# Attention on one core: where the row products stand among the score products of a block

## The reference

```
x: (4, 1024, 1024), D = 1024, 32 heads of 32 columns
h      = layernorm(x) * (1 + ca) + sa
q,k,v  = h @ Wq.T + bq, h @ Wk.T + bk, h @ Wv.T + bv      # split in 32 heads
scores = einsum('bhqd,bhkd->bhqk', q, k) / sqrt(32)
scores = where(causal, scores, -inf)
att    = softmax(scores, axis=-1)
x      = x + ga * (einsum('bhqk,bhkd->bhqd', att, v) @ Wo.T + bo)
h      = layernorm(x) * (1 + cb) + sb
x      = x + gb * experts(h)                               # top 2 of 4, rank 16
```

## Time and profile before

| | |
|---|---|
| three executions | 3041.66, 3042.66, 3043.70 us |
| profiled execution, its own time | 3043.05 us |
| its span, first to last instruction | 3041.3 us |
| granted PE clock from 1302 to 2407 us (in `attend`) | 1.00 |
| in the same 1105 us: PE busy | 1066.65 us |
| DVE, ACT, POOL busy | 737.84, 622.82, 797.86 us |

### The profile page before, as it was taken

The page is one execution under the profiler, slowest core; times in us unless marked ns, Lnnn a source line. Parts: engine busy times, 40 slices in busy tenths (PEclk is TensorE's granted clock), DMA queues, the critical chain, the costliest instruction groups (busy, mean ns, idle before and its releaser), DMA issues. The chain is left out here.

```text
span 3041.3 us, 42552 instructions
## 1 busy us (share of the span) xinstructions
PE 2872.8 (94%) x16692; PEld 2026.8 (67%) x16692; DVE 1528.6 (50%) x3062; ACT 1047.4 (34%) x1443; POOL 1384.0 (46%) x702
## 2 busy tenths in 40 slices
PE   4999999999999999799999999999999959999997
PEld 2788888888888888555555555555555447777775
DVE  4232223222313122366666666666666447777875
ACT  1322321132213111255555555555555521211211
POOL 2322322242225111367776677776777722433342
PEclk8999999999999999899999999999999979999997
DMA  7444343343336444445544444444455163345341
GB/s 240 181 161 161 127 180 111 111 149 128 132 144 194 176 166 151 125 109 120 121 113 112 116 112 112 113 113 112 117 119 120 48 210 110 111 141 156 120 139 42
DMA packets 153935, 404.91 MB, mean 133 GB/s; under 512 B 21756, under 2 KB 57012, under 8 KB 152712
## 3 DMA queue, kind: packets, MB, share of 16 engines
q1 hardware_dynamic: 123416, 292.05, 28.0%
q10 hardware_dynamic: 30320, 110.15, 16.2%
HBM read 270.41 MB, written 131.20 MB: 132 GB/s over the span
## 5 line engine op out<-in xcount | busy, mean ns | idle before, releaser
L1082 ACT ACTIVATE prob<-ps_s 128x1024 f32<-128x1024 f32 (+3 forms) x768 | 598.6, 812 | 471.6 <-PE ps_s L1201 396.1
L782 PE MATMUL ps_u<-h_hi,w_hi 128*128 128x512 f32 x1536 | 620.6, 404 | 1.9 <-POOL h_lo L550 1.6
L782 PE MATMUL ps_u<-h_lo,w_hi 128*128 128x512 f32 x1536 | 608.8, 396 | 0.0
L782 PE MATMUL ps_u<-h_hi,w_lo 128*128 128x512 f32 x1536 | 608.8, 396 | 0.0
L1038 POOL TENSOR_TENSOR added<-added,prob 128x2048 f32<-128x2048 f32 (+1 forms) x128 | 550.0, 4297 | 10.8 <-ACT prob L1082 10.5
L544 POOL TENSOR_TENSOR w_lo<-w_raw,w_hi 128x1024 fp32r<-128x1024 f32 x93 | 222.8, 2396 | 490.2 <-ACT w_hi L612 490.2
L673 DVE SCALAR_TENSOR_TENSOR qk_lo<-ps_u,bias_col,qk_hi 128x512 fp32r<-128x512 f32 x128 | 96.0, 750 | 595.4 <-ACT qk_hi L588 595.4
L1125 DVE TENSOR_REDUCE part_high<-ps_r 128x1 f32<-128x512 f32 x496 | 329.8, 686 | 83.9 <-PE ps_r L1171 75.4
L1121 DVE CUSTOM_DVE_ANT_0 ps_r<-ps_r,row_mask 128x384 f32<-128x384 f32 (+1 forms) x500 | 309.1, 632 | 80.4 <-PE ps_r L1171 68.4
L1171 PE MATMUL ps_r<-k_st,q_st 96*128 96x512 f32 (+1 forms) x1008 | 322.7, 374 | 18.8 <-DMA v_sb<-v_tok 9.2
L782 PEld LDWEIGHTS ps_u<-h_lo,w_hi 128*128 128x128 f32 x1536 | 289.3, 188 | 70.2
(11 more groups left out here) (196 smaller groups left out, 3602.4 us busy)
## 6 DMA issues: line engine op xcount, KB each, us to landing
w_raw<-w_cols SPq DMA_DIRECT2D x72, 512.0 KB, 6.3
qk_split<-qk_hi SPq DMA_DIRECT2D x64, 512.0 KB, 2.6
qk_split<-qk_lo SPq DMA_DIRECT2D x64, 512.0 KB, 4.1
q_st<-qk_split ACTq DMA_DIRECT2D x60, 512.0 KB, 7.6
k_st<-qk_split ACTq DMA_DIRECT2D x60, 512.0 KB, 13.8
xn<-in_L_attn_x SPq DMA_DIRECT2D x8, 2048.0 KB, 13.0
v_tok<-v_out SPq DMA_DIRECT2D x32, 512.0 KB, 4.4
wm<-in_L_wmod SPq DMA_DIRECT2D x8, 2048.0 KB, 7.9
```

Source lines behind the costliest of these rows:

```text
L782: last = nc.tensor.matmul(ps_u[u % 2][:], w[:, m, k], h[:, k, tok], start=k == 0 and j == 0, stop=k == KT - 1 and j == 2)
L1082: nc.scalar.activation(prob[:, buffer_of(t, k), 2 * pair:2 * pair + 2, off:], ps_s[pair][:, :, off:], ACT.Exp, scale=SCALE).then_inc(exp_d ...
```

## The change

The table is another one. Nothing stands in front of the first score pair of a block now; two row products stand in front of the second, of the third and of the fourth; one stands behind the fourth, as before.

```
-    SHARE = (2, 2, 1, 1, 1)
+    SHARE = (0, 2, 2, 2, 1)
```

## The result

The changed kernel takes 3066.47 us (median of six, 3062.24 to 3069.15) against 3042.16 for the kernel before on the same chips (six, 3037.78 to 3044.19). The ratio is 1.0082, interval 1.0069 to 1.0095: slower by 24 us. The forecast was slower, 3061, and the range of 3044 to 3079 holds the result. The profiled execution took 3066.32 us by its own time, with a span of 3064.3.

The account below looks back on a forecast made before the run. Transfers bound block 5, an ACT chain block 2, PE's stream with stops the rest. Terms 0.68 - 0.21 - 0.10 - 0.45 + 0 + 0.70 = +0.62, taken as 0.6 over 30 groups: +18 us, 3061; range 3044 to 3079.

Parts of the forecast that it names:

- Block 3, +0.68: Block 3: waits for DVE's banks make the last row product 1.02 us later, less 0.34 of saved front: +0.68 a group.
- Block 5, +0.70: Block 5: the turn moves behind the first score pair, its 4.56 us transfer chain stays: 5.15 instead of 4.45, +0.70.
- Block 2, 0: Block 2: the ACT chain starts with the first score pair and keeps its length, so no change.
- Block 4, -0.21: Block 4: fourth score pair at 3.50 instead of 3.24, +0.26, less block 5's saved front of 0.47: -0.21 a group.
- block 0, -0.10: Block 0: fourth score pair at 3.09 instead of 2.83, +0.26, less a saved front of 0.36: -0.10 a group.
- Block 1, -0.45: Block 1: fourth score pair stays where ACT lets it go, some 0.02 later, less a saved front of 0.47: -0.45.
- A: Rival, chance 0.10: row products fill PE's holes and DVE keeps up; -0.94 us a group, -28 us, 3015.
- C: Rival, chance 0.13: DVE ends last everywhere, so blocks 0, 1 and 4 save nothing; 1.38 a group, +41 us, 3084.
- B: Rival, chance 0.13: blocks 0, 1 and 4 save their whole fronts, blocks 3 and 5 lose 0.68 and 0.70; +0.08, 3045.
- The transfers: Block 5: the later turn might meet less traffic and win back up to 0.22 a group, some 7 us; left out of sum.

Follow-up runs that it names:

- DVE relieved: Changed kernel with DVE taking single row products' maxima over half of their columns only: 3023.12 us, ratio to the kernel before 0.9936.
- block 3 alone new: Kernel before, with the new table (0, 2, 2, 2, 1) in block 3 only: 3073.54 us, ratio 1.0106.
- block 5 as it was: Changed kernel, with the old table (2, 2, 1, 1, 1) back in block 5: 3063.15 us, ratio to the kernel before 1.0068.
- half DVE work in the kernel before: Kernel before, with DVE taking single row products' maxima over half of their columns: 3030.90 us, ratio 0.9969.
- block 3 as it was: Changed kernel, with the old table (2, 2, 1, 1, 1) back in block 3: 3038.92 us, ratio to the kernel before 0.9986.
- block 5 alone new: Kernel before, with the new table (0, 2, 2, 2, 1) in block 5 only: 3047.09 us, ratio 1.0020.
- the fastest one: Changed kernel with table (1, 2, 2, 1, 1), the turn one place earlier, and own tables for blocks 1, 2 and 3: 2992.78 us, ratio to before 0.9846.
- two transfers: Changed kernel, sending the upper chunk's shift with two transfers instead of four from group 4 on: 3059.34 us, ratio to the kernel before 1.0055.

## Why the prediction was right, point by point

- **Block 3, +0.68: +0.71.** The timetable from DVE's 0.60 us a product gave r4 at 1.51, r6 at 2.60 and S3 at 2.71 after S0; measured 1.52, 2.60 and 2.71. Undone, done alone, and with DVE relieved, it moves as the three banks say. The +0.71 holds the 0.34 of block 4's front; block 3's table by itself costs 1.0 (block 3 alone new).
- **Block 5, +0.70: +0.62 in the mean**, 4.45 to 5.15 between the groups shown. The turn comes 0.60 behind S0 instead of 0.11 ahead, and 4.55 us of DVE, SP and transfer follow. What I didn't see is how near PE's own work was behind it (0.34 us).
- **Block 2, 0: -0.02.** Its chain over ACT starts at S0, but it doesn't quite keep its length: the first exponential starts 0.85 us after S0 instead of 0.98, S1 comes 0.93 behind S0 instead of 1.05, and the median group is 6.57 long instead of 6.68. That the mean moved by 0.02 only is luck: one group of the changed kernel's profile took 8.11 (last section).
- **Block 4, -0.21: -0.16; block 0, -0.10: -0.04.** S3 at 3.53 and 3.16 after S0 in the mean, against 3.50 and 3.09 reckoned. The working has a gap here: DVE's starts of 1.15 and 1.09 don't follow from the 0.34 and 0.69 quoted, which give 1.03 for both, and no row is shown for the rest. The starts measured are 1.16 (2047.19, behind the S0 at 2046.03) and 1.10 (2058.24, behind 2057.14):

```profile
2047.19 0.70 DVE L1121 CUSTOM_DVE_ANT_0 ps_r<-ps_r,row_mask 128x512 f32<-128x512 f32 x1 [1.74 <-PE ps_r L1171]
...
2058.24 0.57 DVE L1121 CUSTOM_DVE_ANT_0 ps_r<-ps_r,row_mask 128x384 f32<-128x384 f32 x1 [1.26 <-PE ps_r L1171]
```

- **Block 1, -0.45: -0.26.** This is the term that was mis-sized. I took S3 to stay where ACT lets it go. But S2 is held by ACT first, and between it and S3 PE now has a product and a product pair with its mask, and the pair waits 0.23 us for a bank. S2, the pair, and S3 of block 1 after the change:

```profile
2066.30 0.30 PEld L1201 LDWEIGHTS ps_s<-slot_q,slot_k 97*128 97x128 f32 x2 [0.23 <-ACT prob L1082]
...
2067.05 0.30 PEld L1171 LDWEIGHTS ps_r<-k_st,q_st 96*128 96x128 f32 x2 [0.23 <-DVE part_high L1125]
...
2067.40 0.31 PEld L1201 LDWEIGHTS ps_s<-slot_q,slot_k 97*128 97x128 f32 x2
```

  1.10 us from S2 to S3, where it was 0.92 before and ACT would allow about that. S3 is at 3.03 after S0 instead of the 2.88 reckoned; with DVE relieved it is at 2.97, so of the 0.15 the bank is 0.06 and PE's own stream 0.09. This term makes 0.19 of the 0.22 a group by which the sum of +0.62 fell short of +0.84.
- **Rivals.** A (DVE keeps up) and C (DVE takes everything) are both out by the table: blocks 1 and 4 did save time, block 3 did lose it. B would need blocks 0, 1 and 4 to save 1.30; they saved 0.46.
- **The transfers.** That they would land more evenly when the turn comes later has weak support: block 5's mean was 0.13 above the 4.45 of an undisturbed group before and is 0.05 above 5.15 after, 2 us in all. In the other profiles it is 0.07 to 0.15 above with the turn in front of S0 (block 3 alone new, block 5 as it was, half DVE work in the kernel before) and 0.05 to 0.09 with the turn behind it (block 3 as it was, block 5 alone new, half DVE work in the changed kernel), so the two overlap. What the prediction cites from the Trainium skill, DMA: Bandwidth & Descriptors, Latency and other measured facts, is said there of HBM, the device memory. In the kernel both ends of these transfers, `shift` and `q_st`, are on-chip buffers, and no run here varies the load on memory, so the reason stays open.

## What to carry to other kernels

Work in front of an engine's wait is worth its time only if it isn't standing in a wait itself, and work moved behind it costs what its receiver's buffers can't take. Here the front of block 3 stood in a wait for ACT, so taking it away saved nothing, and six products among the score pairs, with three banks and 0.60 us each, put S3 0.8 us later: 28 to 32 us for this block's table alone. In blocks 0, 1 and 4 the same six put S3 0.2 to 0.3 us later and saved a front of 0.36 to 0.47. Look also for what else rides in the moved list: one small transpose that starts a 4.5 us chain of transfers came 0.70 us later and so used up the front that was saved there, 5 us net. And one table for six blocks with different limits was not the best here: the block that waits for ACT did better with its filler in front, the others with more of it among the score pairs.

## What the runs showed of the hardware that was not expected

Between 1302 and 2360 us, PE's granted clock fell only in kernels whose block 3 has fewer than two row products in front of S0. In the changed kernel's profile it did once:

```profile
1920.00:1930.00 10.00, 7.61 (x41) 4.18 (x40) 6.29 (x16) 5.32 (x8) 6.84 (x5) 0.96 0.81 187
1930.00:1934.00 4.00, 4.00 (x21) 1.45 (x21) 1.99 (x6) 0.38 (x1) 4.00 (x1) 0.67 1.05 211
1934.00:1945.00 11.00, 10.03 (x71) 5.96 (x71) 8.23 (x22) 5.52 (x8) 6.59 (x7) 1.00 0.52 115
```

(columns: stretch, its length, busy time of PE, PEld, DVE, ACT, POOL, granted clock, transfer share, GB/s). What PE did before:

```profile
1927.02 0.50 PE L1201 MATMUL ps_s<-q_st,k_st 97*128 97x256 f32 x2 [2.15 <-ACT prob L1082]
...
1931.20 2.61 PE L1222 MATMUL ps_o<-prob,v_sb 128*32 128x512 f32 x16
```

It had waited 2.15 us for ACT in front of block 3's S0, where 0.6 is usual in this kernel (ACT's issue of the loads took longer there, 4.9 us instead of the usual 3.65), and then part of the time went at the lower of its two levels, 1.2 GHz: the 16 products of `weigh` took 2.61 us, where 1.92 is what the same ones take in the kernel before. Counted over one profile each between 1302 and 2360 us, such falls were: none in the five kernels with two or three row products in front of block 3 (before, before with half DVE work, block 5 alone new, block 3 as it was, the fastest one); one in the changed kernel, and two to five in each of the six others with none or one. Of the eighteen falls fifteen came in block 3 and made it 1.3 to 1.6 us longer (the changed kernel's was 6.7 long instead of 5.4), one of them 2.6; the other three came in block 0 of the next group and cost about as much there. That block 3's table decides is shown in part: the run with block 3 alone new was expected to have such falls and had three, where the kernel before had none, and block 5 alone new, with block 3 as before, had none. What else it takes is not known, since most groups of the same kernels have no fall. Nor does the single wait decide: with two transfers the five falls came where the load of block 3's S0 had waited 1.5 to 1.8 us, near the usual 1.5, and the longest wait there, 2.68 us, was followed by none.
